# Layer 0 of the first batch with 512-column matmuls over eight PSUM banks, in a two-layer residual kernel

## The reference

```
def _L0(x, W, b, coeff, mask):
    sign = 2 * mask - 1
    return x @ W.T + b + (x @ sign) * coeff
def _L1(x, adapter_mapping, W, b, lora_As, lora_Bs):
    A, Bm = lora_As[adapter_mapping], lora_Bs[adapter_mapping]
    return x @ W.T + b + ((x @ A) @ Bm) * 2.0
x = x + _L0(x, W0, b0, coeff, mask)     # mask: 8 x 1024 x 1024 int32, coeff: one number a batch
x = x + _L1(x, slot, W1, b1, As, Bs)    # slot: which of 32 low-rank adapters a batch uses
```

## Time and profile before

| | |
|---|---|
| median of 3 runs | 392.39 us |
| profiled execution | 392.74 us, of which span 390.9 us |
| PE busy | 382.0 us (98%) |
| DVE busy | 245.9 us (63%) |
| ACT busy | 178.1 us (46%) |
| POOL busy | 49.7 us (13%) |
| transfers | 61.76 MB, 158 GB/s on average |

### The profile page before, as it was taken

How to read it: one execution, slowest core, us unless ns; L and a number is a source line. 1 busy time by engine, 2 the same in 40 slices (tenths; PEclk the granted TensorE clock), 3 DMA queues, 4 the chain that set the end, 5 groups by cost and what they waited for, 6 DMA issues and landing times.

```text
span 390.9 us, 5982 instructions
## 1 busy us (share of the span) xinstructions
PE 382.0 (98%) x2334; PEld 359.1 (92%) x2334; DVE 245.9 (63%) x299; ACT 178.1 (46%) x313; POOL 49.7 (13%) x44
## 2 busy tenths in 40 slices
PE   8879999999999999999999999999999999999997
PEld 8879998998989999989999899899998999998996
DVE  3978989997177932788437981579617794281200
ACT  3546946656155622556235651464515563252221
POOL 2235910020003000030000300012000300002000
DMA  8999817873544633544526436164253562001011
GB/s 288 409 397 364 305 48 223 293 219 108 195 115 161 190 81 135 162 147 157 171 60 196 150 104 216 59 215 140 65 202 111 167 186 106 6 2 54 2 54 55
DMA packets 28078, 61.76 MB, mean 158 GB/s; under 512 B 2554, under 2 KB 3730, under 8 KB 28050
## 3 DMA queue, kind: packets, MB, share of 16 engines
q1 hardware_dynamic: 25232, 52.70, 41.6%
q10 hardware_dynamic: 2754, 8.66, 5.6%
q0 software_dynamic: 64, 0.01, 0.0%
HBM read 52.97 MB, written 8.39 MB: 157 GB/s over the span
## 4 chain that ended last, share of the span: by engine, by line
PE 83%; DVE 6%; DMA 4%; issue 3%; ACT 2%; SPq 1%; ACTq 0%; DVEq 0%
PE z_ps L385 43%; PE y_ps L347 23%; PE y_ps L353 12%; DMA ring<-in_mask 4%; DVE ring L680 3%; PE y_ps L385 2%; PE z_ps L429 2%; DVE wc_lo L688 2%; ACT wc_hi L499 1%; PE y_ps L317 1%; PE y_ps L327 1%; DVE y_two L727 0%; PE t_ps L420 0%; DVE y_raw L721 0%; ACT z_rows L552 0%
## 5 line engine op out<-in xcount | busy, mean ns | idle before, releaser
L385 PE MATMUL z_ps<-w_hi,y_two 128*128 128x344 f32 (+1 forms) x736 | 184.0, 323 | 1.3 <-DVE y_two L727 0.7
L385 PEld LDWEIGHTS z_ps<-w_hi,y_two 128*128 128x128 f32 x736 | 129.5, 188 | 3.0 <-DVE y_two L727 1.0
L347 PE MATMUL y_ps<-x_two,wc_hi 128*128 128x512 f32 x448 | 127.5, 395 | 0.0
L688 DVE SCALAR_TENSOR_TENSOR wc_lo<-ring,coeff_neg,wc_hi 128x1024 fp32r<-128x1024 f32 (+1 forms) x67 | 92.5, 1381 | 47.3 <-ACT wc_hi L499 46.5
L385 PE MATMUL z_ps<-w_lo,y_two 128*128 128x344 f32 (+1 forms) x368 | 118.3, 321 | 0.0
L499 ACT ACTIVATE wc_hi<-ring,coeff_neg 128x1024 fp32r<-128x1024 f32 (+1 forms) x67 | 74.6, 1115 | 71.5 <-PE y_ps L353 37.3
L680 DVE SCALAR_TENSOR_TENSOR ring<-ring,coeff_two,w_t 128x1024 f32<-128x1024 int32 (+1 forms) x67 | 86.6, 1301 | 8.2 <-DMA ring<-in_mask 7.3
L347 PEld LDWEIGHTS y_ps<-x_two,wc_hi 128*128 128x128 f32 x448 | 78.1, 189 | 10.9
L353 PEld LDWEIGHTS y_ps<-x_two,wc_lo 128*128 128x128 f32 x448 | 70.9, 189 | 8.4
L353 PE MATMUL y_ps<-x_two,wc_lo 128*128 128x256 f32 x448 | 78.2, 281 | 0.0
L385 PEld LDWEIGHTS z_ps<-w_lo,y_two 128*128 128x128 f32 x368 | 69.3, 188 | 0.0
(11 more groups left out here) (49 smaller groups left out, 182.3 us busy)
## 6 DMA issues: line engine op xcount, KB each, us to landing
ring<-in_mask SPq DMA_DIRECT2D x63, 512.0 KB, 4.4
x_raw<-in_x SPq DMA_DIRECT2D x31, 256.0 KB, 6.3
out<-z_rows ACTq DMA_DIRECT2D x15, 512.0 KB, 3.2
w_raw<-in_w SPq DMA_DIRECT2D x8, 512.0 KB, 10.3
w_t<-in_w SPq DMA_DIRECT2D x7, 512.0 KB, 9.3
b_raw<-in_lora_b SPq DMA_DIRECT2D x8, 256.0 KB, 3.6
w_t<-in_w SPq DMA_DIRECT2D x2, 256.0 KB, 3.7
ring<-in_mask SPq DMA_DIRECT2D x2, 256.0 KB, 4.8
```

The source lines that it names most:

```text
L347: pe.matmul(y_ps[o % HT][:, 0:2 * T], w, x_two[:, k, :, :], start=(k == 0), stop=False, skip_group_check=True)
L385: ins = pe.matmul(z_bank(b, s, g)[:, 0:EDGES[g + 1] - EDGES[g]], ys[:, k, s * P:(s + 1) * P], w[:, k, EDGES[g]:EDGES[g + 1]], start=(k == ...
L688: dve.scalar_tensor_tensor(out=wc_lo[:, k % RING, lo:hi], in0=sums[:, mask_entry(b, k) % RING, lo:hi], scalar=coeff_neg[:, b:b + 1], in1=w ...
```

## The change

Batch 0 gets the bank layout of the others, except for outputs 0 and 1. `y_bank` puts output o of batch 0 into z_ps0, z_ps1, z_ps2, y_ps0 to y_ps3, t_ps, one bank each. Outputs 0 and 1 keep two 256-column matmuls a block and the direct split from PSUM (`y_high_early`, `y_low_early`). Outputs 2 to 7 get one 512-column matmul a block, and go through y_copy, y_sum, y_high and y_low. y_full now counts every output. Because layer 1's groups lie in banks that layer 0 used, each group's first block waits for that bank's output; the transposition of h in t_ps waits for the last. The order of layer 1's first two blocks changes: block 0 of the three groups of s = 0, then block 1 of these, then both blocks of (1, 0) and of (1, 1).

In the queues of ACT and DVE, x pair 1 is split after the weights of block 1, not ahead of them; on DVE x pairs 2 and 3 are split behind wc_lo of blocks 3 and 5 instead of 2 and 4; and W1 block 1 is split ahead of the first outputs, not behind outputs 0 and 1.

```diff
+        EARLY = 2
+        def y_bank(b, o):
+            if b > 0:
+                return y_ps[o % HT]
+            return (*z_ps, *y_ps, t_ps)[o]
+        def y_sums(b, o):
+            return KT * b + o + 1 - EARLY
+        def y_split(b, k):
+            return k + 1 if b == 0 and k < EARLY else XG * b + k // PAIR + EARLY
...
-                    for n in range(2):
-                        pe.matmul(ys, w, x_two[:, k, n, :], start=(k == 0 and n == 0 and (o == 1 or o % PAIR == 0)),
-                                  stop=False, skip_group_check=True)
+                    if o < EARLY:
+                        for n in range(2):
+                            pe.matmul(y_bank(0, o)[:, 0:T], w, x_two[:, k, n, :], start=(k == 0 and n == 0),
+                                      stop=False, skip_group_check=True)
+                    else:
+                        pe.matmul(y_bank(0, o)[:, 0:2 * T], w, x_two[:, k, :, :], start=(k == 0), stop=False,
+                                  skip_group_check=True)
...
-                    pe.wait_ge(y_lo_done, max(k + 1, PAIR * (g + 1) if s == 1 else 0))
+                    pe.wait_ge(y_lo_done, y_split(0, k))
+                    if k == 0:
+                        o = NG * s + g
+                        if o < EARLY:
+                            pe.wait_ge(y_lo_done, o + 1)
+                        else:
+                            pe.wait_ge(y_sum_done, y_sums(0, o))
...
             w1_high(0)
             lora_a_high(0)
             act.wait_ge(cols_in, 16)
-            for g in range(XG):
-                y_high_first(g)
-                w1_high(g + 1)
-            for k in range(XG + 1, KT):
+            w1_high(1)
+            y_high_early(0)
+            y_high_early(1)
+            y_copy(0, 2)
+            y_copy(0, 3)
+            w1_high(2)
+            y_high(0, 1)
+            y_copy(0, 4)
+            w1_high(3)
+            y_copy(0, 5)
+            y_high(0, 2)
+            w1_high(4)
+            y_copy(0, 6)
+            y_copy(0, 7)
+            y_high(0, 3)
+            for k in range(5, KT):
                 w1_high(k)
...
-            x_low(0, 2)
             for k in range(HALVED, KT):
                 step(0, k)
-                if k == HT:
-                    x_low(0, 3)
+                if k in (3, 5):
+                    x_low(0, (k + 1) // PAIR)
             w1_low(0)
+            w1_low(1)
             dve.wait_ge(cols_in, 16)
-            y_low_first(0)
-            w1_low(1)
-            y_low_first(1)
+            y_low_early(0)
+            y_low_early(1)
+            y_sum(0, 2)
+            y_sum(0, 3)
             w1_low(2)
+            y_low(0, 1)
+            y_sum(0, 4)
             w1_low(3)
-            y_low_first(2)
+            y_sum(0, 5)
+            y_low(0, 2)
             w1_low(4)
-            y_low_first(3)
-            for k in range(XG + 1, KT):
+            y_sum(0, 6)
+            y_sum(0, 7)
+            y_low(0, 3)
+            for k in range(5, KT):
                 w1_low(k)
```

More of the change, by code:

```diff
@@ L171, in block_read @@
             if k == KT - 1 or (b > 0 and k == HT - 1):
-                eng.wait_ge(y_full, y_count(b, k))
+                eng.wait_ge(y_full, KT * b + k + 1)
             elif b == 0:
@@ L324, in layer0_low @@
                         pe.wait_ge(wc_lo_done, parts(0, k, o // HT))
-                    ys = first_bank(o)
                     w = wc_lo[:, k % RING, o * P:(o + 1) * P]
-                    ins = pe.matmul(ys, w, x_two[:, k, 0, :], start=False, stop=(k == KT - 1), skip_group_check=True)
-                    if k == KT - 1 and o % PAIR == PAIR - 1:
+                    ins = pe.matmul(y_bank(0, o)[:, 0:T], w, x_two[:, k, 0, :], start=False, stop=(k == KT - 1),
+                                    skip_group_check=True)
+                    if k == KT - 1:
                         ins.then_inc(y_full, 1)
@@ L333, in bank_free @@
             def bank_free(b, o):
[L335 to L338, removed]
+                if b == 1 and o < 2:
+                    pe.wait_ge(z_done, z_place(0, 1, o))
+                elif b == 1 and o < HT:
+                    pe.wait_ge(y_sum_done, y_sums(0, NG + o))
                 else:
-                    pe.wait_ge(y_sum_done, KT * (b - 1) + o + 1 - HT)
+                    pe.wait_ge(y_sum_done, y_sums(b, o - HT))
             def unit_high(b, u, k, o):
@@ L416, in turn_h @@
                     pe.wait_ge(ones_done, 1)
+                    pe.wait_ge(y_sum_done, y_sums(0, KT - 1))
                 pe.wait_ge(h_hi_done, 2 * (ST * b + s + 1))
@@ L436, in layer1_first @@
                 for k in range(PAIR):
-                    for s, g in ((0, 0), (0, 1), (0, 2), (1, 0)):
-                        first_products(s, g, [k])
+                    for g in range(NG):
+                        first_products(0, g, [k])
+                first_products(1, 0, range(PAIR))
                 first_products(1, 1, range(PAIR))
@@ L512, in x_high, with y_high_early @@
                                ACT.Copy).then_inc(x_hi_done, 1)
[L514 to L519, removed]
+            def y_high_early(o):
+                act.wait_ge(y_full, o + 1)
+                act.activation(y_two[:, 0, o, :], y_bank(0, o)[:, 0:T], ACT.Identity,
+                               bias=b0_cols[:, o:o + 1]).then_inc(y_hi_done, 1)
             def y_copy(b, o):
-                act.wait_ge(y_full, y_count(b, o))
-                if b > 1:
+                act.wait_ge(y_full, KT * b + o + 1)
+                if b > 0:
                     act.wait_ge(y_lo_done, y_split(b - 1, o))
-                act.activation(y_raw[:, o, :], y_ps[o % HT][:, T:2 * T], ACT.Identity,
+                act.activation(y_raw[:, o, :], y_bank(b, o)[:, T:2 * T], ACT.Identity,
                                bias=b0_cols[:, o:o + 1]).then_inc(y_copied, 1)
             def y_high(b, g):
-                act.wait_ge(y_sum_done, KT * (b - 1) + PAIR * (g + 1))
+                act.wait_ge(y_sum_done, y_sums(b, PAIR * g + 1))
                 if g == 0:
@@ L581, in _ @@
             for k in range(KT):
-                if k in (1, 3, 5):
+                if k in (3, 5):
                     x_high(0, (k + 1) // PAIR)
                 weights_high(0, k)
+                if k == 1:
+                    x_high(0, 1)
                 if k == 0:
@@ L706, in x_low, with y_low_early @@
                                   ALU.subtract).then_inc(x_lo_done, 1)
[L708 to L716, removed]
+            def y_low_early(o):
+                dve.wait_ge(y_hi_done, o + 1)
+                dve.scalar_tensor_tensor(out=y_two[:, 1, o, :], in0=y_bank(0, o)[:, 0:T],
+                                         scalar=b0_cols[:, o:o + 1], in1=y_two[:, 0, o, :].bitcast(F32),
+                                         op0=ALU.add, op1=ALU.subtract).then_inc(y_lo_done, 1)
             def y_sum(b, o):
-                dve.wait_ge(y_copied, KT * (b - 1) + o + 1)
-                dve.tensor_tensor(y_raw[:, o, :], y_ps[o % HT][:, 0:T], y_raw[:, o, :],
+                dve.wait_ge(y_copied, y_sums(b, o))
+                dve.tensor_tensor(y_raw[:, o, :], y_bank(b, o)[:, 0:T], y_raw[:, o, :],
                                   ALU.add).then_inc(y_sum_done, 1)
@@ L747, in _ @@
             weights_sum(0, 1, 1)
+            weights_low(0, 1, 0)
             x_low(0, 1)
-            weights_low(0, 1, 0)
             weights_sum(0, 2, 0)
```

7 lines of the change are left out of this document (removed).

## The result

| | before | after |
|---|---|---|
| median of 16 runs | 392.15 us | 393.50 us |
| lowest to highest | 391.74 to 392.84 | 392.18 to 394.79 |
| ratio (95% interval) | | 1.0029 (1.0021 to 1.0037) |
| profiled execution, its span | 392.74, 390.9 us | 393.98, 392.2 us |
| busy: PE, DVE, ACT | 382.0, 245.9, 178.1 us | 381.6, 248.0, 179.9 us |

The change made the kernel slower: by 1.1 us by the ratio, and by 1.35 us between the medians. PE saved 0.4 us of work. DVE and ACT got 2.1 and 1.8 us more.

What follows compares the result with a forecast made beforehand. DVE's packed run from 53.59 us was taken to bound PE's last wait near 90. Delay of 1.8 less 0.33 absorbed gives 1.5, or 1.0; 1.3 was taken: 392.39 + 1.3 = 393.7 us, range 392.5 to 394.8.

Steps and rivals of the forecast that it cites:

- the walk: Stepping through ACT and DVE queues from 36.6 us; delay at x_low(1,1) 1.8 us, less 0.33 absorbed at 58.79.
- the other reading of part 2: At block 7's sum, DVE and POOL do not take turns: +0.1 us instead of +0.5, leaving 1.0 at the end.
- Part 1: Layer 0: wide matmuls save 0.5 us over eight blocks, mostly hidden ahead of the wait ending at 29.03; 0.12 remain.
- Part 2: Layer 0's end: x_low of pair 3 takes turns with POOL's identity add, delaying block 7's sum by 0.5 us.
- The 0.06 and 0.12 us: Small gains set against the x_low delay: 0.06 of a block, 0.12 for y_full counting each output.
- Part 3: W1 block 1 fills DVE's 1.30 us idle before its first y_low; PE starts layer 1 some 0.5 us later.
- Part 4: Evacuation of outputs 2 to 7: DVE gets 1.6 us more work and 2.6 of waits; last w1_low ends at 50.9.
- the upper bound: Cost limit of 3.8 us: no absorption, and five POOL identity adds of 0.4 us each taking turns too.
- Part 5: Ahead of h, x_low, POOL's lora_b_low and the sum run in series until 55.1; x_low(1,1) starts 1.8 us late.
- DVE did not catch up: Rival, chance 0.24: ACT and DVE interlock better, x_low(1,1) within 0.3 us of today; 392.4 to 393.1 us.
- PE did not starve: Rival, chance 0.10: POOL's identity adds delay w1_low, so PE stalls in layer 1; 394.7 to 395.4 us.
- nothing let it be faster: Rival, chance 0.05: PE reaches h 1.0 us earlier with DVE ready for it; 391.4 us.

Runs made afterwards that it cites:

- e5: Kernel before, with lora_b_low of every batch on DVE instead of POOL; 391.44 us, ratio 0.9981.
- e1: Changed kernel, with outputs 2 to 7 of batch 0 multiplied by two 256-column matmuls a block again; ratio 1.0046 to the kernel before.
- e11: Kernel before, with only x_low of pair 3 moved behind wc_lo of block 5; ratio 1.0011.
- e2: Kernel before, with only the moved splits (x pairs 1 to 3 and W1 block 1 at their new places); ratio 1.0004.
- e7: Changed kernel, with W1 block 1 split behind outputs 0 and 1 again on ACT and DVE; ratio 1.0052 to the kernel before.
- e3_wide: Changed kernel, with the moves of x pairs 1 to 3 undone and W1 block 1 still moved; ratio 1.0016 to the kernel before.
- e9: Kernel before, with two more DVE instructions of 0.60 us ahead of x_low(1,0), results not used; ratio 1.0000.
- e8: Kernel before, with four more DVE instructions of 0.60 us ahead of x_low(1,0), results not used; ratio 1.0013.
- e4: Changed kernel, with POOL's lora_b_low in batch 0 handling only 32 of its 1024 columns; ratio 1.0018 to the kernel before.
- e6: Changed kernel, with lora_b_low of every batch on DVE instead of POOL; ratio 0.9995 to the kernel before.
- e10: Changed kernel, with the x pair moves undone and lora_b_low of every batch on DVE; ratio 0.9999 to the kernel before.

## Why the prediction was right

- **The size**: the walk's own figure was 1.8 us late at x_low(1,1) less the 0.33 us, so 1.5; the 1.3 was chosen between this and the 1.0 of the other reading of part 2. In the trace x_low(1,1) is 1.68 us late (55.27 against 53.59). The wc_lo that started at 58.79 starts at 60.06, 1.27 late: 0.41 was absorbed there, and DVE lost or won nothing more up to the last wait. That 1.3 and 1.27 agree to 0.03 us is partly luck.
- **What bounds the kernel**: right. The last wait of PE, on DVE, ended at 91.28 where 91.3 was forecast, and PE had no wait behind it. e5 took it away and gained its 0.7 us.
- **Part 1, wide matmuls hidden**: right, by e1. The distance of 0.23 us held. The 131 ns that the Trainium skill ("TensorE: Matmul & The Clock Gate", back-to-back issue gap) has for a 512-column matmul in such a stream does not occur here.
- **Part 2, x_low of pair 3 against POOL**: right in kind, 0.37 us for 0.5 in size. From the start of x_low to that of the sum it is 0.88 us, where the forecast had 0.60 + 0.40. e11 shows it alone. The 0.06 and 0.12 us that stand against it did not come: DVE's first y_low starts 6.60 us after the sum of block 7, 6.59 before.
- **Part 3, W1 block 1**: PE started layer 1 at 37.05, forecast 37.1. e2 against e11 shows that its new place costs nothing in itself, and e7 that the changed kernel needs it. Of the 0.48 us in A, 0.37 are part 2. The other 0.1 was not foreseen: from the start of DVE's first y_low to PE's first matmul of layer 1 it is 0.73 to 0.75 us in the seven kernels with the new evacuation, and 0.62 or 0.63 in the six others. e1 and e7 have it too, so neither the wide matmuls nor the place of W1 block 1 make it. Its cause stays open.
- **Part 4, the evacuation**: the walk gave 2.6 us of waits and an end at 50.9; the gaps of the trace sum to 0.40 + 2 x 0.70 + 2 x 0.26 = 2.3, and it ended at 51.02. PE did not run dry. The end fits better than the walk: DVE began at 36.32 and not at 36.6 and waited 0.3 us less, but its work took 0.7 us longer. Some 0.5 of that are a y_low (39.38, 0.96 us where the two others take 0.69) and a w1_low (40.60, 1.41 where e3_wide has 1.21), each while POOL was adding an identity; the walk had these turns at nothing, and only the upper bound had them.
- **Part 5, POOL's turn and h**: the sum ended at 55.02 (55.1 forecast) and x_low(1,1) started at 55.27 (55.4). The size of the slack was checked by e9 and e8, and POOL's share by e4. Which instruction POOL would hold up was left open, rightly: it was x_low and not the sum. Of the loss by the distances (1.31), 0.83 us is this part with part 4 (B), 0.37 part 2, and 0.1 the open term above. Neither half of the 0.83 costs anything alone: POOL's turn without the evacuation is hidden in the wait for h (before, e2), and the evacuation without POOL's turn is too (e4).
- **Not foreseen**: the 0.40 us wait of PE at 56.57 for ACT's h_stack. That copy stands behind a wc_hi, which waited for DVE's late sum. It is off the path, as PE had more than that to spare: it still waits 0.83 us at 91.28.
- **The rivals**: DVE did not catch up, PE did not starve, and nothing let it be faster.

## What to carry to other kernels

A faster form of a matmul is worth what the end waits for it: here 48 fewer matmuls moved nothing, while the sums that they made necessary stood just ahead of the stretch where VectorE was the bound. To price added work on such an engine, find the one release that starts its packed run, count its slack there in instructions, and include what other engines take from it by turns. A place that looks free because VectorE waits for GpSimd there need not be: x_low, put into such a wait of 0.42 us, held up what follows by 0.37 us.

## What the runs showed of the hardware that was not expected

**DVE and POOL take turns, and whose turn it is varies.** POOL's 32x1024 subtraction (2.39 us alone) met the sum in the kernel before (3.41 us for 1.28), x_low in the changed one (2.88 for 0.68) and w1_low in e2_moves (3.42 for 1.22). The held-up instruction is longer by 2.1 to 2.2 us in all three. What decides which one it meets, no run here shows.

**The clock after the new evacuation.** Of 72 executions of the seven kernels with the new evacuation (after, e1, e3, e4, e6, e7, e10), 7 have a mean granted clock of 0.996 or less, and they are the slowest of their kernels: 394.13 to 395.29 us, the two of e10 3.2 and 3.3 us above its median. Of 101 executions of the kernel before and 56 of its variants e2, e5, e8, e9 and e11 none has. Only one of the seven was profiled (e7, above), so where the clock falls in the others stays open, and so does why most executions escape it. It adds to the mean of the changed kernel, hardly to its median.
